# The projections of Q, K and V from pairs of F32R numbers to pairs of fp16 numbers behind a power-of-two factor

## The reference

```python
h = einsum('bti,oi->bto', x, W) + bias + 2 * lora(x)            # 8 x 128 tokens, 512 wide
q = (h @ ((qw_q - 8) * repeat(scales_q, 128, axis=0)))          # 32 heads of 128
k = (h @ ((qw_k - 8) * repeat(scales_k, 128, axis=0)))          # 8 heads of 128
v = (h @ ((qw_v - 8) * repeat(scales_v, 128, axis=0)))          # 8 heads of 128
attn = softmax(causal(rope(q) @ rope(k).T / sqrt(128)))         # four q heads share one k and v
x = x + (attn @ v) @ ((qw_o - 8) * repeat(scales_o, 128, axis=0))
x = x + ffn(lora2(x))                                           # layer norm, two int8-rounded layers
```

## Time and profile before

| | |
|---|---|
| median of 3 runs | 567.71 us (567.18 to 568.55) |
| span of the profiled execution, first to last instruction | 567.4 us |
| TensorE matmul busy | 544.6 us, 96% |
| VectorE busy | 485.5 us, 86% |
| ScalarE busy | 362.8 us, 64% |
| GpSimd busy | 400.2 us, 71% |
| mean granted TensorE clock | 0.997 |

### The profile page before, as it was taken

How to read it: one execution, slowest core, us unless ns; L and a number is a source line. 1 busy time by engine, 2 the same in 40 slices (tenths; PEclk the granted TensorE clock), 3 DMA queues, 4 the chain that set the end, 5 groups by cost and what they waited for, 6 DMA issues and landing times.

```text
span 567.4 us, 10591 instructions
## 1 busy us (share of the span) xinstructions
PE 544.6 (96%) x3183; PEld 431.7 (76%) x3187; DVE 485.5 (86%) x627; ACT 362.8 (64%) x939; POOL 400.2 (71%) x410
## 2 busy tenths in 40 slices
PE   8999989999999999999999999999999999987985
PEld 6654778878888888888888888888888888864432
DVE  2753859998999899979997999799979998976997
ACT  2574476656665766576657665766576657556795
POOL 3005677799679977997799779977997799761053
PEclk9999999999999999999999999999999999999899
DMA  8932526412541254125422542154224312200003
GB/s 297 230 85 56 153 70 168 112 43 63 156 103 49 60 160 99 51 59 153 104 54 55 149 110 55 55 141 118 52 59 129 92 43 69 57 0 2 0 20 129
DMA packets 38173, 51.93 MB, mean 92 GB/s; under 512 B 12101, under 2 KB 20453, under 8 KB 38149
## 3 DMA queue, kind: packets, MB, share of 16 engines
q1 hardware_dynamic: 35652, 46.94, 31.5%
q10 hardware_dynamic: 2016, 3.48, 2.0%
q0 software_dynamic: 480, 1.22, 0.7%
HBM read 28.55 MB, written 2.10 MB: 54 GB/s over the span
## 4 chain that ended last, share of the span: by engine, by line
PE 82%; DVE 9%; issue 2%; ACT 2%; POOL 2%; DMA 2%; SPq 0%; DVEq 0%; ACTq 0%; POOLq 0%
PE pair L1389 23%; PE pair L1390 23%; PE flow L1378 9%; PE flow L1506 9%; PE flow L1498 4%; PE pair L1307 2%; DVE raw_v L1072 1%; PE flow L1383 1%; PE pair L1324 1%; PE flow L1307 1%; DVE y_max L1182 1%; DMA swap_q<-raw_q 1%; DVE ctx_lo L1093 1%; DVE probs L1194 1%; DVE rope_c L1194 1%
## 5 line engine op out<-in xcount | busy, mean ns | idle before, releaser
L1086 DVE SCALAR_TENSOR_TENSOR accT<-pair,so_now,accT 128x1024 f32<-128x1024 f32 x125 | 157.3, 1275 | 13.7 <-PE pair L1390 12.9
L1072 DVE SCALAR_TENSOR_TENSOR raw_q<-pair,sc_now,raw_q 128x1024 f32<-128x1024 f32 x90 | 115.4, 1283 | 6.3 <-ACT raw_q L769 2.9
L562 POOL TENSOR_TENSOR probs<-probs,rowinv 128x512 f32<-128x512 f32 x64 | 66.7, 1043 | 64.7 <-DVE rowinv L1059 64.6
L714 ACT ACTIVATE probs<-flow,negmax 128x128 f32<-128x128 f32 x248 | 87.6, 368 | 32.8 <-DVE negmax L1040 32.8
L1389 PE MATMUL pair<-ctx_hi,wo 128*128 128x512 f32 x256 | 104.9, 410 | 2.7 <-issue 1.5
L1390 PE MATMUL pair<-ctx_lo,wo 128*128 128x512 f32 x256 | 100.3, 392 | 0.0
L1389 PE MATMUL pair<-h_hi,wq 128*128 128x512 f32 x240 | 99.9, 416 | 0.0
L1390 PE MATMUL pair<-h_lo,wq 128*128 128x512 f32 x240 | 94.1, 392 | 0.0
L531 POOL TENSOR_TENSOR rope_s<-swap_q,consts 128x512 f32<-128x512 f32 x62 | 80.2, 1293 | 9.9 <-DMA swap_q<-raw_q 9.9
L543 POOL TENSOR_TENSOR qT<-rope_c,rope_s 128x512 f32<-128x512 f32 x62 | 79.4, 1280 | 4.4
L531 POOL TENSOR_TENSOR rope_c<-raw_q,consts 128x512 f32<-128x512 f32 x62 | 78.8, 1294 | 0.0
(11 more groups left out here) (243 smaller groups left out, 977.7 us busy)
## 6 DMA issues: line engine op xcount, KB each, us to landing
swap_q<-raw_q SPq DMA_DIRECT2D x62, 256.0 KB, 3.7
wq_i<-in_L_attn_qw_q SPq DMA_DIRECT2D x8, 1024.0 KB, 5.9
wo_i<-in_L_attn_qw_o SPq DMA_DIRECT2D x32, 256.0 KB, 2.7
swap_k<-raw_k SPq DMA_DIRECT2D x14, 256.0 KB, 3.6
wkv_i<-in_L_attn_qw_k SPq DMA_DIRECT2D x8, 256.0 KB, 3.6
wkv_i<-in_L_attn_qw_v SPq DMA_DIRECT2D x8, 256.0 KB, 4.0
stage<-in_x ACTq DMA_DIRECT2D x4, 256.0 KB, 4.8
probs<-in_L_ffn_w ACTq DMA_DIRECT2D x4, 256.0 KB, 7.2
```

The costliest lines, as they stand in the source:

```text
L562: pool.tensor_tensor(pr, pr, rowinv[:, f, :].unsqueeze(2).broadcast_to([P, HB, P]), ALU.mult).then_inc(probs_done, 1)
L714: e = act.activation(probs[:, 0, f, seq(b)], bank[:, seq(b)], ACT.Exp, bias=negmax[:, f, b:b + 1], accum_out=rowsum[:, f, b:b + 1])
L1072: dve.scalar_tensor_tensor(out=into, in0=flat(pair[pair_of(h, (kind, j), last, first)][:, :, :]), scalar=sc_now[:, scale_slot(kind, h), j: ...
L1086: dve.scalar_tensor_tensor(out=a, in0=flat(pair[pair_of(h, (O, c), last, first)][:, :, :]), scalar=so_now[:, (h if c == 0 else h - 1) % 2, ...
```

## The change

h is held as a pair of fp16 numbers, h times a factor, and the weights of Q, K and V (whole numbers from -8 to 7) are held in fp16. The factor is a power of two, worked out on the chip: the largest absolute values of x, W, the bias and the two adapter tables are found by VectorE along the free side, turned by TensorE so that the maximum across partitions can be taken, and spread to all partitions by a small product. From them comes a bound on h, whose exponent gives `unit` and `gain` = 1 / unit. ScalarE writes h times gain as f32 into `h_scaled` (one half of the tokens), and VectorE makes both fp16 numbers out of it. The scales of Q, K and V are multiplied by `unit` once. Output products, scores and context stay as they are.

```diff
-        h_hi = sb("h_hi", [P, C, T], F32R)
-        h_lo = sb("h_lo", [P, C, T], F32R)
+        h_hi = sb("h_hi", [P, C, T], F16)
+        h_lo = sb("h_lo", [P, C, T], F16)
+        h_scaled = sb("h_scaled", [P, C, HALF])
-        wkv = sb("wkv", [P, 2, C, P], F32R)
+        wkv = sb("wkv", [P, 2, C, P], F16)
-        wq = sb("wq", [P, 2, C, P], F32R)
+        wq = sb("wq", [P, 2, C, P], F16)
...
# GpSimd, before it copies the first scales
-            pool.wait_ge(scT_kept, 4)
+            pool.wait_ge(scales_in_unit, 1)
...
# ScalarE
                 act.wait_ge(strips_done, C * (HB * f + HB - 1) + c + 1)
-                act.activation(h_hi[:, c, half[f]], linear_bank(k), ACT.Identity, bias=bias_col[:, c:c + 1]).then_inc(hi_made, 1)
+                if f:
+                    act.wait_ge(lo_made, c + 1)
+                act.activation(h_scaled[:, c, :], linear_bank(k), ACT.Identity, bias=bias_gained[:, c:c + 1],
+                               scale=gain[:, 0:1]).then_inc(h_gained, 1)
...
-            act.wait_ge(d_bias, 16)
+            act.wait_ge(gain_made, 1)
             for k in range(C):
                 keep_upper(k)
...
# VectorE
+            def peak(into, source, *landed):
+                for w in landed:
+                    dve.wait_ge(w, 16)
+                return dve.tensor_reduce(into, source, AX.X, ALU.max, apply_absolute_value=True)
+
+            def peak_of_weights(i):
+                peak(W_peaks[:, i:i + 1], flat((raw_q, raw_k)[i][:, :, :]), d_w[2 * i], d_w[2 * i + 1])
+
+            def peaks_of_x():
+                peak(x_peaks[:, 0:1], stage[:, :, :].rearrange("p b n -> p (b n)"), *d_x[0:HB])
+
+            def peaks_of_late_x():
+                peak(x_peaks[:, 1:2], flat(raw_v[:, :, :]), d_x[4], d_x[5])
+                link(peak(x_peaks[:, 2:3], v_flat, d_x[6], d_x[7]))
+                peak(peaks[:, PEAK_X:PEAK_X + 1], x_peaks[:, :])
+                peak(peaks[:, PEAK_W:PEAK_W + 1], W_peaks[:, :])
+                peak(peaks[:, PEAK_BIAS:PEAK_BIAS + 1], bias_col[:, :], d_bias)
+
+            def peaks_of_adapters():
+                dve.wait_ge(d_la, 16 * 2 * B)
+                peak(peaks[:, PEAK_A:PEAK_B + 1], qT[:, 0, :].rearrange("p (m n) -> p m n", m=2)).then_inc(peaks_made, 1)
+
+            def spread_tops():
+                dve.wait_ge(peaks_turned, 1)
+                link(dve.tensor_reduce(peak_top[:, :], banks[5][0:N_PEAKS, 0:P], AX.X, ALU.max))
+                dve.tensor_scalar(peak_diag[:, :], ident[0:N_PEAKS, 0:N_PEAKS], peak_top[:, 0:1], None, ALU.mult).then_inc(tops_made, 1)
+
+            def make_gain():
+                ...
+                dve.wait_ge(tops_spread, 1)
+                link(dve.tensor_copy(tops[:, :], banks[5][:, P:P + N_PEAKS]))
+                link(dve.tensor_scalar(bound[:, :], top(PEAK_A), top(PEAK_B), 2.0 * R, ALU.mult, ALU.mult))
+                link(dve.tensor_scalar(bound[:, :], bound[:, :], top(PEAK_W), top(PEAK_X), ALU.add, ALU.mult))
+                link(dve.tensor_scalar(bound[:, :], bound[:, :], float(D), top(PEAK_BIAS), ALU.mult, ALU.add))
+                link(dve.tensor_scalar(bound[:, :], bound[:, :], BOUND_MOST, BOUND_LEAST, ALU.min, ALU.max))
+                link(dve.tensor_scalar(bound[:, :].bitcast(I32), bound[:, :].bitcast(I32), EXPONENT_BITS, None, ALU.bitwise_and))
+                link(dve.tensor_scalar(unit[:, :], bound[:, :], UNIT_OF_BOUND, None, ALU.mult))
+                link(dve.reciprocal(gain[:, :], unit[:, :]))
+                dve.tensor_scalar(bias_gained[:, :], bias_col[:, :], gain[:, 0:1], None, ALU.mult).then_inc(gain_made, 1)
+                dve.wait_ge(scT_kept, 4)
+                by_column = sc_cols[:, :, :].rearrange("p h c -> p (h c)")
+                dve.tensor_scalar(by_column, by_column, unit[:, 0:1], None, ALU.mult).then_inc(scales_in_unit, 1)
...
+            def make_upper(k):
+                f, c = k // C, k % C
+                dve.wait_ge(h_gained, k + 1)
+                dve.tensor_copy(h_hi[:, c, half[f]], h_scaled[:, c, :]).then_inc(hi_made, 1)
+            def make_lower(k):
+                f, c = k // C, k % C
                 dve.wait_ge(hi_made, k + 1)
-                dve.scalar_tensor_tensor(out=h_lo[:, c, half[f]], in0=linear_bank(k), scalar=bias_col[:, c:c + 1],
-                                         in1=h_hi[:, c, half[f]], op0=ALU.add, op1=ALU.subtract).then_inc(lo_made, 1)
+                dve.tensor_tensor(h_lo[:, c, half[f]], h_scaled[:, c, :], h_hi[:, c, half[f]], ALU.subtract).then_inc(lo_made, 1)
...
             find_scale(0)
+            peaks_of_x()
             keep_x(5, banks[5])
             keep_x(7, banks[7])
             find_scale(1)
-            for k in range(2, 5):
+            for k in range(2, 4):
                 clip_weights(k - 2)
                 find_scale(k)
+            peaks_of_late_x()
+            clip_weights(2)
+            find_scale(4)
             clip_weights(3)
+            keep_scales()
+            peaks_of_adapters()
+            clip_weights(4)
             find_scale(5)
-            keep_scales()
-            clip_weights(4)
+            spread_tops()
             keep_lora_rows()
+            make_gain()
             find_scale(6)
             clip_weights(5)
-            for k in range(C):
-                keep_rest(k)
+            split_half(0)
...
# TensorE
             lora_rows()
+            pe.wait_ge(peaks_made, 1)
+            pe.transpose(banks[5][0:N_PEAKS, 0:P], peaks[:, :], ident).then_inc(peaks_turned, 1)
             pe.wait_ge(scT_kept, 4)
             turn_weights(2)
+            pe.wait_ge(tops_made, 1)
+            pe.matmul(banks[5][:, P:P + N_PEAKS], ones[0:N_PEAKS, :], peak_diag[:, :], start=True, stop=True).then_inc(tops_spread, 1)
             linear_lora(0)
...
             linear(4)
+            pe.wait_ge(gain_made, 1)
             linear(5)
```

More of the change, by code:

```diff
@@ L33 @@
 EPS = 1e-5
+PEAK_X, PEAK_W, PEAK_BIAS, PEAK_A, PEAK_B, N_PEAKS = 0, 1, 2, 3, 4, 5
+BOUND_LEAST, BOUND_MOST = 2.0 ** -100, 2.0 ** 126
+EXPONENT_BITS = 0x7F800000
+UNIT_OF_BOUND = 2.0 ** -14
 TINY = 1e-8
@@ L114, in build @@
         bias_col = sb("bias_col", [P, C])
+        bias_gained = sb("bias_gained", [P, C])
+        x_peaks, W_peaks = sb("x_peaks", [P, 3]), sb("W_peaks", [P, 2])
+        peaks = sb("peaks", [P, N_PEAKS])
+        peak_diag = sb("peak_diag", [N_PEAKS, N_PEAKS])
+        peak_top = sb("peak_top", [N_PEAKS, 1])
+        tops = sb("tops", [P, N_PEAKS])
+        bound = sb("bound", [P, 1])
+        unit, gain = sb("unit", [P, 1]), sb("gain", [P, 1])
         ffT = sb("ffT", [P, 2, C, D], BF16)
@@ L182, in build @@
         u_done, u_kept, strips_done = sem("u_done"), sem("u_kept"), sem("strips_done")
-        hi_made, lo_made = sem("hi_made"), sem("lo_made")
+        h_gained, hi_made, lo_made = sem("h_gained"), sem("hi_made"), sem("lo_made")
+        peaks_made, peaks_turned = sem("peaks_made"), sem("peaks_turned")
+        tops_made, tops_spread = sem("tops_made"), sem("tops_spread")
+        gain_made, scales_in_unit = sem("gain_made"), sem("scales_in_unit")
         ff_top, ff_rounded, ff_clipped = sem("ff_top"), sem("ff_rounded"), sem("ff_clipped")
@@ new lines, in spread_tops, with top @@
+            def spread_tops():
[3 more added lines that the diff above has]
+            def make_gain():
+                def top(n):
+                    return tops[:, n:n + 1]
+                dve.wait_ge(tops_spread, 1)
[11 more added lines that the diff above has]
+                dve.tensor_scalar(by_column, by_column, unit[:, 0:1], None, ALU.mult).then_inc(scales_in_unit, 1)
@@ L965, in _ @@
                 dve.tensor_copy(WT[:, :, seq(c)], banks[4 + c].rearrange("p (c n) -> p c n", c=C)).then_inc(WT_dve, 1)
+                if c in (1, 2):
+                    peak_of_weights(c - 1)
             def keep_scales():
@@ L981, in keep_lora_rows, with split_half @@
                                   lora_parity[:, :].unsqueeze(2).broadcast_to([P, 2, P]), ALU.mult).then_inc(u_kept, 1)
-            def keep_rest(k):
+            def make_upper(k):
[3 more added lines that the diff above has]
+            def make_lower(k):
                 f, c = k // C, k % C
                 dve.wait_ge(hi_made, k + 1)
-                dve.scalar_tensor_tensor(out=h_lo[:, c, half[f]], in0=linear_bank(k), scalar=bias_col[:, c:c + 1],
-                                         in1=h_hi[:, c, half[f]], op0=ALU.add, op1=ALU.subtract).then_inc(lo_made, 1)
+                dve.tensor_tensor(h_lo[:, c, half[f]], h_scaled[:, c, :], h_hi[:, c, half[f]], ALU.subtract).then_inc(lo_made, 1)
+            def split_half(f):
+                make_upper(C * f)
+                for k in range(C * f, C * f + C):
+                    if k < C * f + C - 1:
+                        make_upper(k + 1)
+                    make_lower(k)
             dve.wait_ge(d_tables, 16)
@@ L1044, in _ @@
             early_groups(Q, 1, 0)
-            for k in range(C, 2 * C):
```

(2 more changed lines are left out.)

## The result

The changed kernel takes 573.23 us (median of 4 runs, 572.19 to 577.06) against 568.13 us before. The ratio is 1.010, with a 95% interval of 1.0071 to 1.0129, so it is slower, and the time lies above the prediction's range (564.0 to 571.5). The ratio is the one on record for all runs of both kernels; by the two medians alone it would be 1.009. The profiled execution has a span of 571.5 us against 567.4. The two profiles differ by 4.1 us, and the ratio stands for 5.7. Part of this lies in the profile before: in every run whose span is on record the time is 1.8 to 3.1 us above the span, so the execution profiled there took over 569 us, more than each of the four runs it stands beside. The four runs of the changed kernel had mean granted clocks of 0.990 to 0.993, the profiled one 0.993.

The account below looks back on a forecast made before the run. Each group was taken as bounded by TensorE for some 14.4 us and VectorE for 42.6. Loop -4.6, start +4.1 and clock +1.0 gave +0.5 us: 567.7 to 568.2 us, no change that can be told; range 564.0 to 571.5.

Parts of the forecast that it names:

- The bound: Start: VectorE's reductions delay the adapters' rows, so TensorE's lora strips and linear(4) wait, +3.1 us.
- The clock: Start, lora strips and linear(4): one fall to the lower clock level for 3.4 us after sparse TensorE work, +1.0 us.
- fp16's gain in the loop: Loop over eight head groups: faster Q, K and V matmuls, 0.55 us a steady group, -4.6 us in all.
- the clock stays low for longer: Start: short strips may not restore the clock; it costs 2.7 us in place of 1.0, 569.9 us; chance 0.27.
- The last rival: Loop: fp16 runs at F32R's pace, so the loop gives 0 and the time is 572.8 us; chance 0.07.
- Q3's and K's savings: Loop: time saved in steps between turn and context (Q3: 0.05 + 0.09 us) is lost in their fixed 1.36 us distance.
- VectorE's arc: Part of each group where VectorE sets the time, 42.6 us; of 1.3 us idle, 0.3 was expected as gain.
- The bound of -18.8: Loop: the most it could gain, TensorE's whole saving from matmul pace (9.5) and extra time behind short matmuls (9.3).
- the first rival: Loop: TensorE keeps the lead and most of 2.7 us a group arrives, 559 us; chance 0.12.
- the second split: Start: splitting h's second half into two fp16 numbers lies on the path, +1.2 us, bounds 0.5 and 1.9.
- the start is covered: Start: reductions find slack, only half of 3.1 us shows and the clock holds, 565.6 us; chance 0.16.
- the 0.5 that the prediction gave for this rule: Start: shared SBUF ports make VectorE's first copy wait for GpSimd's q addition, 0.5 us later, 568.7 us.

Follow-up runs that it names:

- the second order: Changed kernel with the adapters' rows first, then maxima, spread and gain in one go, feed-forward weight rounding behind them: 576.29 us, ratio 1.0100.
- the kernel with filling and two tiles: Changed kernel plus two sets of twelve unread filling products and a second tile for the query's sum, used in turn: 567.06 us, ratio 0.9975.
- The kernel before with two tiles: Kernel before, F32R throughout, with a second tile for the query's sum, used in turn: 567.55 us, ratio 0.9974.
- the delay with 14 products: Kernel before with three unused reductions ahead of the copy of the adapters' rows, and 14 unread filling products on TensorE: 569.34 us, ratio 1.0024.
- Three orders: Changed kernel with the adapters' rows copied first and the start's work in three different orders: ratios 1.0112, 1.0100 and 1.0076 to the kernel before.

## Why the prediction was wrong

By the ratios the change splits into four terms, each the difference between two kernels that were run; each has some 1 to 2 us of uncertainty, and they add up to the whole by the way they are formed. fp16: -1.9 (predicted -4.8). The split with a constant factor: +0.6 (predicted +1.2). The bound, with the clock held by filling: 1.0030 - 0.9976, +3.1 (predicted +3.1). The clock: 1.0100 - 1.0030, +4.0 (predicted +1.0). The sum is +5.7, where I had +0.5. Two terms failed, by about as much: the clock by 3.0 us and fp16's gain in the loop by 2.9.

**The clock** was priced too low. The prediction placed the fall rightly, between 32 and 37 and on the strips and `linear(4)`, and named the emptiness of the stretch as the cause; filling it showed that to be so. It took the length from the one fall that the trace had, 3.4 us, though it said that the new stretch was emptier; the clock stayed low for 6.8. How sparse the stretch is doesn't set the length by itself: behind 3.8 us of idle TensorE the kernel with the second order had only 3.4 us of it. The prediction also took the price from four short bf16 matmuls. The strips lost 0.7 and the sixteen products 2.3 us: 3.0 in the profile. The rival "the clock stays low for longer" had the mechanism and a chance of 0.27, but stopped at 2.7 us; with fp16 at the measured -1.9 it would have come to 569.9 + 2.9 = 572.8. The last rival, fp16 at the pace of F32R, also had 572.8, next to the measured 573.23. That is luck: its mechanism didn't occur, as the pace fell to 0.216. The last 1 us between the profile and the ratio is not settled; more falls in other executions are likely, as mean clocks of 0.990 were seen, but I have no profile of those runs.

**The loop** failed through a wait that the prediction didn't have. The pace is 0.216 us (eight matmuls from 236.75 to 238.48), near the assumed 0.213, and the extra 0.09 behind short matmuls is gone. That Q3's and K's savings are lost in the distance from the turn to the context was right: the two turns of head 3 lie 2.28 us apart before and 2.29 after. What was wrong is "on VectorE's arc the idle time is 1.3 us; I give 0.3". It left out who else uses the tile that the faster steps fill. The Q step came earlier, ScalarE was free earlier to drain it, and GpSimd's cosine had not yet read the last one. Without that wait the gain of the period was 56.94 - 56.47, 0.47, and that of the kernel 4.4 us by the ratios, close to the forecast of 0.55 and 4.8; in the profiles the stretch to the last drain of V3 gained 3.1 (0.4 and 2.7), where the forecast had 4.1 (0.8 and 3.3). The bound of -18.8 is a slip of the sum (704 x 0.014 is 9.9, so -19.2); it moves only the first rival, by 0.3. The prediction had weighed TensorE and VectorE against each other, and not the order in which ScalarE and GpSimd use `raw_q`.

**The start.** Rows of one cause fit well: one reduction over 1024 took 1.21 us as estimated, the adapters' rows came 2.85 us later than the lora rows explain (predicted 3.1), the gain's chain and the first split were covered. In the profile the second split took 1.6 us more (60.79 to 65.04, against 54.27 to 56.91 before), for a predicted 1.2 with bounds of 0.5 to 1.9. Its own figures (3.7, 2.73 and 0.1) give 1.1, and VectorE's casts and subtractions do take 3.75 us where all copies are ready (35.45 to 39.20 in the kernel with filling and two tiles). The other 0.5 are a wait for ScalarE's second copy and the cast that is told of below. The runs put only 0.6 on the split. The rest of the 8.0 us is 1.1 us by which the lora rows were already late: in this execution four turns of x or W take 1.06 us still at 9.27 and 0.60 from 11.27 on, in the profile before they take 1.06 us still at 6.57 and 0.60 from 8.84 on. The granted clock reads 1.00 there in both. The kernel before with two tiles, whose start is unchanged, has 1.06 at 6.63 and 0.60 at 9.24, and the delay with 14 products 0.60 already at 5.66, so this differs from execution to execution. Behind the loop the order was reversed: the fall of the earlier trace rows is missing in the profile after.

The prediction held the chance that the start is covered at 0.16 and leaned on VectorE's idle time. Three orders showed that it isn't covered, whichever work is put off. The shared ports did show, where the prediction had put them. GpSimd's addition of q ran from 60.15 to 61.42 (timeline of GpSimd), and VectorE's first cast of the second split began at 60.79 within it, as soon as ScalarE's copy was ready. The lengths of the eight casts (ns, shortest, middle and longest), and the timeline of VectorE up to 61.3:

```profile
60.15 1.27 POOL L513 TENSOR_TENSOR qT<-rope_c,rope_s 128x512 f32<-128x512 f32 x1 [1.46 <-PE flow L1400]
```

```profile
L1055 DVE CAST h_hi<-h_scaled x8: 412/422/911, 37.7 to 63.5; 128x512 f16<-128x512 f32 x8
```

```profile
60.79 0.91 DVE L1055 CAST h_hi<-h_scaled 128x512 f16<-128x512 f32 x1 [6.35 <-ACT h_scaled L684]
```

That one cast took 0.91 us and ended at 61.70; the others took 0.41 to 0.43. In the profiles of all eight kernels with this cast, in F32R and with a constant factor too, the cast that begins within GpSimd's addition takes 0.91 or 0.92 and the other seven at most 0.43. By the rule of the Trainium skill, SBUF — State Buffer, section SBUF: two separate sides, the cast would have waited until 61.42, and with its 0.42 have ended at 61.84. The trace agrees with it within 0.14 us. It doesn't tell waiting from a slower pace during the overlap, as the cast begins 0.63 or 0.64 us into the addition each time. The price was small: VectorE would have waited for ScalarE's second copy meanwhile, and the split took 4.25 us against 4.09 for the first one (37.74 to 41.83), 0.16 more and not the 0.5 that the prediction gave for this rule.

## What to carry to other kernels

Work that makes TensorE wait 1.2 us twice can cost more than the 2.4 us of waiting: look at what runs behind the gap, and price it at half the clock, also for longer than the one example in the trace, or fill the gap with products that nobody reads, sized to end when the wait does. When an engine gets faster, go through the tiles that it and its drains write, and ask for each who has still to read the last contents: here one more tile was worth 2.3 us in the profiles and 4.0 by the ratios, where the faster matmuls on their own had shown 1.9. Before moving work out of the way in a crowded start, look at what the moved-back work feeds next, and at which queues are in order.

## What the runs showed of the hardware

- After a sparse stretch (1.6 us busy in 4.0) the granted clock was at 1.2 GHz for 6.8 us, with F32R and with fp16. After milder ones (0.81 busy in 2.0, or 2.37 in 4.0) it was there for 3.4 us, but after 3.8 us of idle TensorE too. Which of the two lengths comes isn't shown.
- A VectorE cast of 128x512 from f32 that began 0.64 us into a GpSimd addition took 0.91 us (0.92 at most) in place of 0.42, in eight profiles of eight.
- An fp16 matmul of 128x512 follows another at 0.216 us with a weight load of 98 ns; in F32R it was 0.2275 us, with a load of 189 ns.
- One kernel, run twelve times, had mean clocks from 0.995 to 1.0 and times from 565.91 to 569.38 us, the longer ones mostly at the lower clocks; a difference of 1 us between single profiles of such a kernel tells nothing.
